# Expert layer: each step's down product issued two steps behind its up product, with a ring of three PSUM banks

## What is computed

```python
logits = jnp.einsum('th,eh->te', x, gate_w)
probs = jax.nn.softmax(logits, axis=-1)
topk_w, topk_idx = jax.lax.top_k(probs, TOP_K)
topk_w = topk_w / jnp.sum(topk_w, axis=-1, keepdims=True)
...
g = jnp.einsum('th,ehi->tei', x, w1)
u = jnp.einsum('th,ehi->tei', x, w3)
act = jax.nn.silu(g) * u
expert_out = jnp.einsum('tei,eih->teh', act, w2)
out = jnp.einsum('teh,te->th', expert_out, scores)
...
x = _layernorm(x + out)
```

## Time and profile before

| | us |
|---|---|
| median of 3 runs (419.38, 419.49, 422.47) | 419.49 |
| the profiled execution: its own time | 421.96 |
| the profiled execution: span in the trace | 420.0 |
| mean granted clock of TensorE in it | 0.955 |
| PE matmuls busy in the span | 363.9 (87%) |
| DVE, ACT, POOL busy in the span | 277.1, 227.5, 217.1 |
| first gate product of the experts to the end of the last down product | 317.2 to 412.8 |

### The profile page before, as it was taken

One profiled execution on the slowest core, in us unless ns is written; L12 is line 12 of the kernel. 1 busy time (PEld: TensorE's weight loads), 2 busy tenths in 40 slices (PEclk: granted clock), 3 DMA queues, 4 the chain that ended last, 5 costly groups with the idle time before them and its releaser, 6 DMA issues. The chain is left out here.

```text
span 420.0 us, 11906 instructions
## 1 busy us (share of the span) xinstructions
PE 363.9 (87%) x3620; PEld 261.0 (62%) x3620; DVE 277.1 (66%) x1296; ACT 227.5 (54%) x495; POOL 217.1 (52%) x403
## 2 busy tenths in 40 slices
PE   2695878899989999888598999999888989999992
PEld 1673656667666677666476777777663745566661
DVE  6553978888888889886354767767763245644443
ACT  1426467678877877657548667676353242222220
POOL 8639244677766776567475332331113335355542
PEclk9977599999999999999779999999999989999998
DMA  6877676656666666532424334333004520163300
GB/s 130 232 141 140 155 123 129 124 112 130 130 129 120 126 134 123 89 47 57 107 66 108 90 92 109 92 83 95 2 2 150 181 75 2 35 198 108 118 25 25
DMA packets 50427, 43.40 MB, mean 103 GB/s; under 512 B 21776, under 2 KB 43104, under 8 KB 48848
## 3 DMA queue, kind: packets, MB, share of 16 engines
q1 hardware_dynamic: 49344, 42.29, 44.1%
q0 software_dynamic: 512, 0.48, 0.9%
q10 hardware_dynamic: 528, 0.10, 0.1%
HBM read 32.24 MB, written 10.62 MB: 102 GB/s over the span
## 5 line engine op out<-in xcount | busy, mean ns | idle before, releaser
L1452 DVE CUSTOM_DVE_ANT_0 bank<-bank,decayed_e 128x128 f32<-128x128 f32 x256 | 66.8, 322 | 1.0
L635 POOL TENSOR_TENSOR stk<-stk 128x512 f32<-128x512 f32 x32 | 40.6, 1269 | 45.8 <-ACT stk L1309 43.7
L1463 DVE TENSOR_REDUCE top<-bank 128x4 bf16<-128x512 f32 x64 | 44.2, 691 | 30.2 <-PE bank L721 30.0
L1102 ACT ACTIVATE prob<-bank 128x512 f32<-128x512 f32 x64 | 38.2, 597 | 32.4 <-PE bank L700 31.8
L1700 DVE TENSOR_TENSOR stk<-bank,stk 128x512 f32<-128x512 f32 x32 | 22.1, 691 | 50.5 <-POOL stk L635 50.4
L1441 DVE TENSOR_TENSOR decayed_e<-bank,decay 128x512 f32<-128x512 f32 x64 | 43.9, 686 | 16.9 <-issue 16.5
L1309 ACT ACTIVATE stk<-bank 128x512 f32<-128x512 f32 x32 | 19.0, 597 | 60.3 <-PE bank L1013 60.3
L471 POOL TENSOR_TENSOR rest<-pf,parts 128x512 f32<-128x512 f32 (+1 forms) x32 | 29.2, 914 | 40.2 <-ACT parts L1091 40.2
L1026 PEld LDWEIGHTS bank<-w,stk 128*128 128x128 f32 x256 | 33.4, 192 | 22.0 <-DVE stk L1700 14.5
L477 POOL TENSOR_TENSOR parts<-rest,parts 128x512 bf16<-128x512 f32 (+1 forms) x32 | 29.3, 915 | 26.7 <-ACT parts L1095 26.7
L768 PE MATMUL bank<-prob_t,vmix 128*16 128x128 f32 x768 | 39.4, 278 | 0.1
(11 more groups left out here) (204 smaller groups left out, 829.5 us busy)
## 6 DMA issues: line engine op xcount, KB each, us to landing
stk<-parts_dram SPq DMA_DIRECT2D x128, 64.0 KB
stk<-shares_dram SPq DMA_DIRECT2D x64, 128.0 KB, 3.0
parts_dram<-parts SPq DMA_DIRECT2D x16, 384.0 KB, 5.4
stk<-parts_dram SPq DMA_DIRECT2D x112, 32.0 KB
stk<-parts_dram SPq DMA_DIRECT2D x16, 192.0 KB
parts_dram<-parts SPq DMA_DIRECT2D x16, 192.0 KB, 2.4
stk<-parts_dram SPq DMA_DIRECT2D x16, 128.0 KB
w<-in_L_ffn_w_dram SPq DMA_DIRECT2D x3, 512.0 KB, 13.0
```

Of the source, the lines that this page charges most:

```text
L635: pool.tensor_tensor(h1[kk % 2], sg[kk % 2], share[kk], ALU.mult).then_inc(weighted, 1)
L1102: act.activation(prob[g % 2][:].rearrange("p h t -> p (h t)"), bank[g % 2][:], ACT.Exp).then_inc(L.exped, 1)
L1452: m = dve.tensor_tensor_reduce(out=bank[g % 2][:, 128 * j:128 * j + 128], in0=bank[g % 2][:, 128 * j:128 * j + 128], in1=decayed_e[:, g % ...
L1463: dve.tensor_reduce(top[:, b.par, GH * g:GH * g + GH], bank[0][:].rearrange("p (h t) -> p h t", h=GH), AX.X, ALU.max).then_inc(L2.maxed, 1)
```

## The change

PE issues D(u-2) behind U(u), in place of D(u-1), and the last two down products behind the last step. The up products go round three banks, 2, 3 and 6, and `actt` has three buffers. U(u) now waits for V(u-3), and V(u) for D(u-3). DVE's `finish` parts stand one step later, behind V of kk = 2 and 4, and POOL's root behind W of kk = 3. The rings of `sg`, `h1` and the gate banks stay two deep, and the work put between the steps on PE, DVE and ACT stays at its (c, kk).

```diff
-        actt = [scratch[:, TC * (4 + p):TC * (5 + p)] for p in range(2)]
+        actt = [scratch[:, TC * (4 + p):TC * (5 + p)] for p in range(3)]
...
+        UP_BANK = (2, 3, 6)
...
-                    if kk == 2 and (not isinstance(c, int) or c >= 1):
+                    if kk == 3 and (not isinstance(c, int) or c >= 1):
                         final_root(c - 1)
...
-                if late:
-                    pe.wait_ge(glu, u - 1)
-                pe.matmul(bank[2 + kk % 2][:], w3[:, 128 * kk:128 * kk + 128], xt, start=True, stop=True
+                if u >= 3:
+                    pe.wait_ge(glu, u - 2)
+                pe.matmul(bank[UP_BANK[u % 3]][:], w3[:, 128 * kk:128 * kk + 128], xt, start=True, stop=True
                           ).then_inc(up_mm, 1)
...
-                    m = pe.matmul(bank[4 + c % 2][:, 128 * t:128 * t + 128], actt[kk % 2][:, 128 * t:128 * t + 128],
+                    m = pe.matmul(bank[4 + c % 2][:, 128 * t:128 * t + 128], actt[u % 3][:, 128 * t:128 * t + 128],
...
-                    if kk >= 1:
-                        down_product(c, kk - 1)
-                    elif not isinstance(c, int) or c >= 1:
-                        down_product(c - 1, KC - 1)
+                    u = c * KC + kk - 2
+                    if u >= 0:
+                        down_product(u // KC, u % KC)
...
+            down_product(NCH - 1, KC - 2)
             down_product(NCH - 1, KC - 1)
...
-                if not isinstance(u, int) or u >= 2:
-                    dve.wait_ge(down, u - 1)
-                dve.tensor_tensor(actt[kk % 2], bank[2 + kk % 2][:], h1[kk % 2], ALU.mult).then_inc(glu, 1)
+                if u >= 3:
+                    dve.wait_ge(down, u - 2)
+                dve.tensor_tensor(actt[u % 3], bank[UP_BANK[u % 3]][:], h1[kk % 2], ALU.mult).then_inc(glu, 1)
...
-                    if kk in (1, 3) and (not isinstance(c, int) or c >= 1):
-                        finish(c - 1, kk // 2)
+                    if kk in (2, 4) and c >= 1:
+                        finish(c - 1, kk // 2 - 1)
```

## The result

The changed kernel took 417.88 us (median of 18 runs, 412.92 to 419.73), the kernel before, measured again beside it, 420.80 us (18 runs, 418.17 to 422.59). The ratio is 0.9911, 95% interval 0.9883 to 0.9939. The kernel is 0.7 to 0.9% faster. That is inside the range of 414.4 to 418.7 and on the side forecast, but 1.9 us over the forecast itself, and outside the 415.0 to 416.8 of rival A, on which the forecast rests. The profiled execution took 418.22 us, with a span of 416.3 (before: 421.96 and 420.0).

The account below looks back on a forecast made before the run. PE's own work bounds the steady stretch; stalls elsewhere go. 0.35 + 2.0 + 1.8 + 1.4 = 5.5 us off the profiled 421.96 gives 416.4, or 3.75 off the 419.49 median gives 415.7; taken 416.0, range 414.4 to 418.7.

Parts of the forecast that it names:

- rival A: Whole kernel: stalls go and the new gap leaves the clock up; 416.0 us, own range 415.0 to 416.8; chance 0.42.
- What bounds the steady steps: Steps 16 to 30: PE's own work is the limit, step stays 2.61 us, gain 0.
- Place 1: Steps 0 to 3: wait moved to one gap of 2.0 to 2.1 us before the x2 transposes; gain 0.35 us.
- Place 2: Step 6, D(6) waiting for late V(6): stall gone, gain 2.0 us, plus 1.8 us of clock.
- Place 3: Steps 10 to 13, V late on DVE: slack of 3.1 us covers the lateness; gain 1.4 us.
- rival C: Chunk 1: stalls return as DVE lateness, V(11) over 3.1 us late; 417.4 to 418.5, with the clock 419.5; chance 0.13.
- Place 4: Last step: the chain still sets the end, D(31) ready 3.84 us after G(31); gain 0.
- The clock: the unknown: Behind the new gap at 324.3: the clock may fall or not, costing 0 to 1.8 us; taken as 0.
- Rival B: Clock falls behind the new gap at 324.3, G(3) to about D(2) at 1.2 GHz; 417.5 us; chance 0.30.
- D: Steady steps gain after all, since weight loads are busy only 62%; 413 to 415.3 us; chance 0.10.
- E: Chunk 2: share loads come late behind the store of chunk 0; 424 us; chance 0.05.
- the 3.75 forecast for that case: Whole kernel: gain in us if the median runs had no clock fall at step 6, giving 415.7 us.

Follow-up runs that it names:

- e8_both: Changed kernel with x2 transposes at step 3, finish and root two steps later, share loads ahead of the store; 413.12 us, ratio 0.984.
- e1_gap: Changed kernel with both groups of x2 transposes at step 3, so PE goes on with G(3); 414.45 us, ratio 0.986.
- e5_before_fill: Kernel before with two extra unused matmuls behind U(7), where PE stands for V(6); 420.25 us, ratio 1.000.
- e11_finish_only: Kernel before with only finish and POOL's root moved back one step, lag one, rings of two; 419.41 us, ratio 1.001.
- e3_two_banks: Changed kernel with up products on two banks, U(u) waiting for V(u-2), lag of two and three actt buffers kept; 415.49 us, ratio 0.988.
- e6_light_route: Changed kernel with stages 2 to 4 of the second half's routing replaced by eleven one-column memsets; 416.12 us, ratio 0.989.
- e4: Changed kernel with finish and POOL's root back in their old places; 419.30 us, ratio 0.997.
- e0_after: The changed kernel run again, unaltered, for a second execution of its trace; 416.70 us, ratio 0.992 to the kernel before.
- e7: Changed kernel with D(u-1) behind U(u) again; three up banks, three actt buffers and later finish kept; 420.35 us, ratio 1.001.

## Why the prediction was right, and where it was off

**What bounds the steady steps: right.** G14 to G31 is 44.37 us, 17 steps of 2.61, in every kernel. The sentence on LDWEIGHTS from the Trainium skill ("Perfetto Trace Analysis", "Identifying the Most-Contended Engine") didn't hold here: LDWEIGHTS is busy 55.07 of 86.90 us (63%) in e8_both, where nothing is left to close between the matmuls.

**Place 1: the mechanism right, the size near.** Forecast a gap of 2.0 to 2.1 us before the first transposes, and G(3) 0.35 earlier against the chain. Measured 2.15; G0 to G3 is 9.81 us against 9.93 before, 0.1 earlier. The part was under-read in another way: I called the gap moved and let it be, while e1_gap shows that it costs its whole length, 2.4 us from start to start.

**Place 2: right.** No wait at D(6): G(8) to G(12) is 10.44 us, four plain steps. The stall of 2.0 is gone, and so is the low clock behind it, which was worth 1.5 us and not 1.8 (e5_before_fill). This stall is all that the lag itself removed: from e11_finish_only to e3_two_banks G0 to G8 falls by 2.34 us, and G8 to G14 by 0.1.

**Place 3: the step that failed in part.** Forecast 1.4 us. G8 to G12 gave its 0.6, which is owed to the later `finish` and not to the slack, since e11_finish_only has the same 10.44 us with a lag of one. G12 to G14 is 6.19 for 6.11 before: nothing of the 0.8. The failed sentence is "DVE works some 13 of 21 us, so it catches up". The meetings with POOL were in the sum, but the average over the chunk was not the right test: DVE starts already 2.5 us late with V(6) and has no idle time until V(12). "Lateness at one V stays at two meetings and one block of work, under 3 us" was wrong with it: V(11) was 3.8 us late, behind four meetings. That is rival C in a mild form, a wait of 0.7 us, and e3_two_banks and e6_light_route show the cause.

**Place 4: right.** 3.84 us from G(31) to D(31), before and after.

**The clock: the unknown went the other way in the traces.** Rival B, priced at 1.8 us, was seen twice in the changed kernel's traces, at 1.7 us. The clock stayed up in e3, e4 and e6 at the same gap. Which it is in how many of the 18 executions, no run here settles.

**The sum of the profiled execution.** Forecast 5.5 us less than before, measured 421.96 - 418.22 = 3.7. The experts gave 94.40 - 91.61 = 2.8: 5.5, less 1.7 for the clock, 0.8 for V(11) and 0.2 at place 1. The rest, 1.0, is G(0) starting at 316.2 in place of 317.2, which the change does not touch.

**The median.** Forecast 3.5 us less than 419.49, measured 2.9 less than 420.80. 1.3 of the 1.9 us by which 416.0 was too low is the reference: three runs had put the kernel before 1.3 us lower than eighteen. I had also explained the 2.5 us between its profiled execution and its median by the clock at step 6. Such a choice can't be made from one trace: e5_before_fill took that drop out of the trace and the median stayed. By the columns with the clock up the change is worth 92.90 - 89.9 = 3.0 us, which agrees with the medians: the 3.75 forecast for that case, less the 0.8 of V(11). That the time still fell in the range is in part luck. The range was wide enough for A and B together, A itself missed, and nothing in the working foresaw the reference. (The 0.33 given to "D, and half of A" sums to 0.31.)

**Rivals D and E fell.** The steady step stayed at 2.61 us. W(16) was released by its Silu. W(24), at 387.64, is put down to its shares in the changed kernel's trace, but it starts 1.88 us behind its G, as W(16) does there and in the kernel before, and PE waited for nothing.

**Which part of the change did it.** By the columns, with the clock up: 92.90 before, 91.96 with only `finish` moved, 89.53 with the lag and the third `actt` too, 89.9 with the third bank as well. The lag is worth 2.4 us, but only with `finish` moved: with `finish` left in its place (e4_finish) it is worth 0.2.

## What to carry to other kernels

More slack on an engine that is already full in the steady stretch pays only where some other engine is late, so count the late places one by one, and then ask what stands next in the list of the engine set free: it runs sooner into its next wait (here 2.15 us for `x2`). Moving that work behind what is ready was worth another 2.4 us, as much as the lag, and the third bank was worth nothing before both repairs were in. When an engine is late for a stretch, test its idle time from the first lateness on, not its average load. And a short instruction that waits for a late engine (here POOL's root) holds all that stands behind it in its queue. Here no V waited for the W that it held; the W came to lie beside other DVE instructions and held those.

## What was not expected of the hardware

The clock fell behind a gap of the matmuls of about 2 us in some executions and not in others of the same length: of eight profiled executions with the gap left unfilled at V(6) or at the `x2` transposes (1.7 to 2.3 us), it fell in four (before, changed, e0_after, e7) and stayed up in four (e3, e4, e6, e11). The gaps of the first four are 1.85 to 2.15 us, those of the other four 1.73 to 2.29, so the length doesn't decide it. The price was 1.5 to 1.7 us each time.

A copy of 8 columns on DVE took 1.18 us beside a W of POOL, in place of 0.17: it ended at 348.66, with the W at 348.64. The copy of 32 columns ended at 351.28, its W at 351.25. In e3_two_banks a copy of 16 columns began 0.49 us before the end of a W and took 0.52. In these three the delay goes by how much of the W is left, and not by the size of the copy.
